# An attention stage in which weighing moves a step later, queries and keys are projected apart, and VectorE takes two copies from ScalarE

## The reference

```python
q = (inputs @ w_q.T).reshape(b, t, H, HD)      # b = 4, t = 256, H = 16 heads, HD = 16
k = (inputs @ w_k.T).reshape(b, t, H, HD)
v = (inputs @ w_v.T).reshape(b, t, H, HD)
scores = jnp.einsum('bqhd,bkhd->bhqk', q, k)
scores = jnp.where(causal, -jnp.inf, scores)
scale = jnp.float32(t) ** 0.5
attn = jax.nn.softmax(scores / scale, axis=-1)
ctx = jnp.einsum('bhqk,bkhd->bqhd', attn, v).reshape(b, t, D)
return ctx @ w_o.T + b_o
```

## Time and profile before

| what | value |
|---|---|
| median of three runs | 420.56 us |
| profiled execution | 420.87 us, span 419.1 us |
| PE busy | 380.4 us, 91% |
| DVE busy | 296.6 us, 71% |
| ACT busy | 256.6 us, 61% |
| POOL busy | 237.5 us, 57% |
| chain that ended last | PE 57%, DMA 16%, DVE 15%, ACT 3%, POOL 2% |

### The profile page before, as it was taken

The page is one execution under the profiler, slowest core; times in us unless marked ns, Lnnn a source line. Parts: engine busy times, 40 slices in busy tenths (PEclk is TensorE's granted clock), DMA queues, the critical chain, the costliest instruction groups (busy, mean ns, idle before and its releaser), DMA issues.

```text
span 419.1 us, 9185 instructions
## 1 busy us (share of the span) xinstructions
PE 380.4 (91%) x2732; PEld 309.0 (74%) x2733; DVE 296.6 (71%) x620; ACT 256.6 (61%) x640; POOL 237.5 (57%) x307
## 2 busy tenths in 40 slices
PE   7769999999999989788888988797899999999996
PEld 3548888888888867566666766473788888888885
DVE  6878999555666796887777757967466765566566
ACT  2837865656555546799888878621455556555552
POOL 5255445565567359567878668201555545745860
PEclk9999999999999999899999989999999999999999
DMA  7949921112111620466867587819721111112126
GB/s 253 399 125 391 379 97 54 52 38 75 50 50 38 238 77 0 76 114 116 151 117 129 103 108 145 139 20 305 238 96 55 53 62 52 50 50 57 43 96 231
DMA packets 70929, 51.57 MB, mean 123 GB/s; under 512 B 53104, under 2 KB 64624, under 8 KB 70640
## 3 DMA queue, kind: packets, MB, share of 16 engines
q1 hardware_dynamic: 66064, 36.99, 34.3%
q0 software_dynamic: 4544, 12.07, 9.3%
q10 hardware_dynamic: 288, 2.10, 1.3%
HBM read 29.37 MB, written 9.19 MB: 92 GB/s over the span
## 4 chain that ended last, share of the span: by engine, by line
PE 57%; DMA 16%; DVE 15%; issue 4%; ACT 3%; POOL 2%; SPq 1%; DVEq 0%; ACTq 0%; POOLq 0%
PE bank L1408 27%; PE bank L1430 13%; DMA pT<-parts 5%; DMA w_raw<-in_win_t 4%; PE bank L1418 4%; PE bank L1580 3%; DMA pT<-parts_late 3%; PE bank L1547 3%; PE bank L1384 2%; DMA w_out<-y_scratch 2%; DVE x L1097 2%; DMA y_scratch<-arena,scatter_row 2%; DVE neg_max L1200 1%; PE bank L1617 1%; DVE parts L1214 1%
## 5 line engine op out<-in xcount | busy, mean ns | idle before, releaser
L546 POOL DMA_INDIRECT arena<-xn_scratch,gather_row x46 | 49.6, 1078 | 68.1 <-PE bank L1384 46.7
L552 POOL DMA_INDIRECT y_scratch<-arena,scatter_row x42 | 62.5, 1488 | 37.1 <-ACT arena L715 35.3
L1408 PE MATMUL bank<-w_hi,xT_hi 128*128 x184 | 61.7, 416 | 0.4 <-ACT xT_hi L674 0.4
L1058 DVE TENSOR_TENSOR wo_lo<-w_out,wo_hi 128x1024 fp32r<-128x1024 f32 x46 | 56.3, 1224 | 3.8 <-PE bank L1430 2.2
L1063 DVE TENSOR_TENSOR gT_lo<-bank,gT_hi 128x512 fp32r<-128x512 f32 x46 | 31.7, 690 | 38.1 <-ACT gT_hi L689 38.1
L1408 PE MATMUL bank<-w_hi,xT_lo 128*128 x184 | 57.5, 393 | 0.0
L1408 PE MATMUL bank<-w_lo,xT_hi 128*128 x184 | 57.3, 392 | 0.0
L682 ACT ACTIVATE arena<-bank 128x512 f32<-128x512 f32 x46 | 27.6, 599 | 45.6 <-PE bank L1408 45.6
L627 POOL TENSOR_TENSOR k_head<-k_hi,head_mask 128x256 fp32r<-128x256 f32 x64 | 38.7, 626 | 24.3 <-PE bank L1581 24.3
L704 ACT ACTIVATE wo_hi<-w_out 128x1024 fp32r x46 | 48.8, 1061 | 5.1 <-issue 3.0
L1580 PE MATMUL bank<-k_head,xT_hi 128*128 128x256 f32 (+1 forms) x128 | 40.2, 395 | 7.7 <-DVE parts L1214 5.9
(11 more groups left out here) (196 smaller groups left out, 915.5 us busy)
## 6 DMA issues: line engine op xcount, KB each, us to landing
w_raw<-in_win_t SPq DMA_DIRECT2D x8, 1024.0 KB, 10.9
w_out<-in_wout_t SPq DMA_DIRECT2D x16, 512.0 KB, 7.6
w_out<-y_scratch SPq DMA_DIRECT2D x8, 512.0 KB, 5.3
xn_scratch<-arena ACTq DMA_DIRECT2D x2, 1024.0 KB, 6.2
x<-in_x SPq DMA_DIRECT2D x4, 256.0 KB, 3.4
out<-x SPq DMA_DIRECT2D x4, 256.0 KB, 2.2
arena<-xn_scratch,gather_row POOLq DMA_INDIRECT x46, 3.4
y_scratch<-arena,scatter_row POOLq DMA_INDIRECT x46, 3.0
```

The lines of the kernel that those rows point to most:

```text
L546: pool.indirect_dma_start(out=xb[j % 2][:, :], out_offset=None, in_=xn_dram, in_offset=bass.IndirectOffsetOnAxis(ap=gather_row[:, j:j + 1] ...
L552: pool.indirect_dma_start(out=y_dram, in_=y[j % 2][:, :], in_offset=None, out_offset=bass.IndirectOffsetOnAxis(ap=scatter_row[:, j:j + 1], ...
L1058: dve.tensor_tensor(wo_lo[:, :, :], w_out[:, bass.ds(e, 1), :, :].rearrange("p o c d -> p (o c) d"), wo_hi[u][:, :, :].bitcast(F32), ALU.s ...
L1408: last = pe.matmul(bank[2 * half + u][:, :], tok[u][:, k, :], wts[:, bass.ds(e, 1), k, half * H:(half + 1) * H], start=(part == 0 and k == ...
```

## The change

Weighing moves from the end of step s + 3 to step s + 4, ahead of the projections and the head scores; the last call of `step` gets a sixth inner step, and its matmuls on ones go from 6 to 5 a step. `chunk` is parted into `key_chunk` (steps 0 and 3, bank 7) and `query_chunk` (steps 1 and 4, bank 4). VectorE and no longer ScalarE makes `q_hi` and copies the turned context. The summing up of banks 5 and 6 is parted and lies in step 5 around the head maximum and head low part, with the reciprocal alone at the end of step 4. The turned context and the output projection use bank 4; the projection is parted around the tail scores of step 7. The values leave bank 4 and alternate between banks 5 and 6.

```diff
@@ -55,20 +55,20 @@
-VBANK = (3, 4, 5, 6, 5, 6, 5, 6)
+VBANK = (3, 5, 6, 5, 6, 5, 6, 5)
...
-CHUNK_STEP = (0, 3)
+KEY_STEP, QUERY_STEP = (0, 3), (1, 4)
...
-WARM_END = 6
+WARM_END = 5
@@ -378,7 +379,7 @@
-            return range(HPAIRS if new else SUM_STEP)
+            return range(HPAIRS if new else SLAG + 4)
@@ -791,13 +792,11 @@
-            def chunk(b, c):
...
-                act.wait_ge(qk_done, b * DK + (c + 1))
-                reach(act, head_scored, b * HPAIRS + (CPAIRS * (c + 1) - HPAIRS))
-                act.activation(k_hi[:, c, :], bank[7][:, SEQ:2 * SEQ], ACT.Copy).then_inc(k_hi_ready, 1)
-                act.activation(q_hi[c][:, :, :], bank[7][:, 0:SEQ].rearrange("p (q t) -> p q t", q=2), ACT.Copy,
-                               scale=1.0 / SEQ ** 0.5).then_inc(qk_hi_ready, 1)
+            def key_chunk(b, c):
...
+                act.wait_ge(k_done, b * DK + (c + 1))
+                reach(act, k_head_ready, b * HPAIRS + (CPAIRS * (c + 1) - HPAIRS))
+                act.activation(k_hi[:, c, :], bank[7][:, 0:SEQ], ACT.Copy).then_inc(k_hi_ready, 1)
@@ -839,18 +838,14 @@
                 for s in steps_of(new):
-                    if old and s == OUT_STEP:
-                        act.wait_ge(ctxT_done, b)
-                        act.activation(ctxT[:, :, :], bank[7][:, :].rearrange("p (k t) -> p k t", k=DK), ACT.Copy,
-                                       scale=1.0 / P_SCALE).then_inc(ctxT_ready, 1)
...
                         turn_out(1, (1,))
-                    if new and s in CHUNK_STEP:
-                        chunk(b, CHUNK_STEP.index(s))
+                    if new and s in KEY_STEP:
+                        key_chunk(b, KEY_STEP.index(s))
@@ -1181,14 +1176,21 @@
-            def chunk(b, c):
...
-                dve.wait_ge(qk_hi_ready, b * DK + (c + 1))
-                dve.tensor_tensor(k_lo[:, c, :], bank[7][:, SEQ:2 * SEQ], k_hi[:, c, :].bitcast(F32), ALU.subtract)\
+            def key_chunk(b, c):
...
+                dve.wait_ge(k_hi_ready, b * DK + (c + 1))
+                dve.tensor_tensor(k_lo[:, c, :], bank[7][:, 0:SEQ], k_hi[:, c, :].bitcast(F32), ALU.subtract)\
                     .then_inc(k_lo_ready, 1)
-                dve.scalar_tensor_tensor(q_lo[c][:, :, :], bank[7][:, 0:SEQ].rearrange("p (q t) -> p q t", q=2),
-                                         1.0 / SEQ ** 0.5, q_hi[c][:, :, :].bitcast(F32),
-                                         ALU.mult, ALU.subtract).then_inc(qk_ready, 1)
...
+            def query_chunk(b, c):
...
+                scaled = bank[4][:, 0:SEQ].rearrange("p (q t) -> p q t", q=2)
+                dve.wait_ge(q_done, b * DK + (c + 1))
+                reach(dve, head_scored, b * HPAIRS + (CPAIRS * (c + 1) - HPAIRS))
+                dve.tensor_scalar(q_hi[c][:, :, :], scaled, 1.0 / SEQ ** 0.5, None, ALU.mult).then_inc(q_hi_ready, 1)
+                dve.wait_ge(q_hi_ready, b * DK + (c + 1))
+                dve.scalar_tensor_tensor(q_lo[c][:, :, :], scaled, 1.0 / SEQ ** 0.5, q_hi[c][:, :, :].bitcast(F32),
+                                         ALU.mult, ALU.subtract).then_inc(q_ready, 1)
@@ -1214,19 +1216,23 @@
-            def add_up(b):
...
-                sums = row_sum[:, bass.ds(b - 1, 1), :, :].rearrange("p o q h -> p (o q) h")
+            def invert(b):
...
+                sums = row_sum[:, b - 1, :, :]
+                dve.wait_ge(high_ready, b * HEADS)
+                reach(dve, ctx_ready, b - 1)
+                dve.reciprocal(inv_sum[:, :, :], sums).then_inc(inv_ready, 1)
...
+            def add_up(b, qt):
...
                 dve.wait_ge(pv_done, b * HEADS)
-                for qt in range(2):
-                    dve.tensor_reduce(ctxv[:, qt, :, :], bank[5 + qt][:, :].rearrange("p (h w d) -> p h d w", w=2, d=HD),
-                                      AX_X, ALU.add).then_inc(ctx_summed, 1)
-                dve.reciprocal(inv_sum[:, :, :], sums).then_inc(inv_ready, 1)
+                dve.tensor_reduce(ctxv[:, qt, :, :], bank[5 + qt][:, :].rearrange("p (h w d) -> p h d w", w=2, d=HD),
+                                  AX_X, ALU.add).then_inc(ctx_summed, 1)
...
                 rows = x[:, bass.ds(b * 2 - 2, 2), :]
-                dve.tensor_tensor(rows, rows, bank[7][:, :].rearrange("p (q d) -> p q d", q=2), ALU.add)\
+                dve.tensor_tensor(rows, rows, bank[4][:, :].rearrange("p (q d) -> p q d", q=2), ALU.add)\
@@ -1247,18 +1253,28 @@
                 for s in steps_of(new):
-                    if old and s == SUM_STEP:
-                        add_up(b)
...
                         low(b, s, True)
+                    if old and new and s == SUM_STEP:
+                        add_up(b, 0)
...
                         maxima(b, s, False)
-                    if new and s in CHUNK_STEP:
-                        chunk(b, CHUNK_STEP.index(s))
+                    if new and s in KEY_STEP:
+                        key_chunk(b, KEY_STEP.index(s))
+                    if new and s in QUERY_STEP:
+                        query_chunk(b, QUERY_STEP.index(s))
...
                         low(b, s, False)
+                    if old and new and s == SUM_STEP - 1:
+                        invert(b)
+                    if old and new and s == SUM_STEP:
+                        add_up(b, 1)
+                    if old and new and s == OUT_STEP:
+                        dve.wait_ge(ctxT_done, b)
+                        dve.tensor_scalar(ctxT[:, :, :], bank[4][:, :].rearrange("p (k t) -> p k t", k=DK), 1.0 / P_SCALE, None,
+                                          ALU.mult).then_inc(ctxT_ready, 1)
@@ -1535,23 +1551,29 @@
-            def chunk(b, c):
...
-                if c:
-                    pe.wait_ge(qk_ready, b * DK + c)
-                else:
+            def key_chunk(b, c):
...
+                reach(pe, k_lo_ready, b * DK + c)
+                for k in range(DK):
+                    last = pe.matmul(bank[7][:, 0:SEQ], wk[:, k, c * P:(c + 1) * P], xnT[:, k, b * SEQ:(b + 1) * SEQ],
+                                     start=(k == 0), stop=(k == DK - 1))
+                last.then_inc(k_done, 1)
...
+            def query_chunk(b, c):
...
+                reach(pe, q_ready, b * DK + c)
+                if c == 0:
                     reach(pe, attn_added, b)
-                for w, to in ((wq, 0), (wk, SEQ)):
-                    for k in range(DK):
-                        last = pe.matmul(bank[7][:, to:to + SEQ], w[:, k, c * P:(c + 1) * P], xnT[:, k, bass.ds(b * SEQ, SEQ)],
-                                         start=(k == 0), stop=(k == DK - 1))
-                last.then_inc(qk_done, 1)
+                for k in range(DK):
+                    last = pe.matmul(bank[4][:, 0:SEQ], wq[:, k, c * P:(c + 1) * P], xnT[:, k, b * SEQ:(b + 1) * SEQ],
+                                     start=(k == 0), stop=(k == DK - 1))
+                last.then_inc(q_done, 1)
...
-                    reach(pe, v_rest_ready, t - 1 if t >= 4 else 0)
+                    reach(pe, v_rest_ready, t - 1 if t >= 3 else 0)
@@ -1566,7 +1588,7 @@
-                        pe.wait_ge(qk_ready, b * DK + (c + 1 - (DK if s < SLAG else 0)))
+                        pe.wait_ge(q_ready, b * DK + (c + 1 - (DK if s < SLAG else 0)))
@@ -1583,12 +1605,12 @@
-                g = b * HPAIRS + (s - SLAG - 3)
-                ago = s < SLAG + 3
-                turned = pT[(s - 1) % 2]
+                g = b * HPAIRS + (s - SLAG - 4)
+                ago = s < SLAG + 4
+                turned = pT[g % 2]
...
                 for hh in range(2):
-                    h = 2 * ((s - SLAG - 3) % HPAIRS) + hh
+                    h = 2 * ((s - SLAG - 4) % HPAIRS) + hh
@@ -1603,25 +1625,25 @@
-                    pe.wait_ge(qk_ready, b * DK + DK)
+                    pe.wait_ge(q_ready, b * DK + DK)
...
                         heads = ctxv[:, qt, c * HPC:(c + 1) * HPC, :].rearrange("p h d -> p (h d)")
-                        last = pe.transpose(bank[7][:, c * SEQ + qt * P:c * SEQ + (qt + 1) * P], heads, ident[:, :])
+                        last = pe.transpose(bank[4][:, c * SEQ + qt * P:c * SEQ + (qt + 1) * P], heads, ident[:, :])
...
-            def project_out(b):
+            def project_out(b, qt):
                 pe.wait_ge(ctxT_ready, b)
-                for qt in range(2):
-                    for c in range(DK):
-                        last = pe.matmul(bank[7][:, qt * D:(qt + 1) * D], ctxT[:, c, qt * P:(qt + 1) * P], wo[:, c, :],
-                                         start=(c == 0), stop=(c == DK - 1))
-                last.then_inc(o_done, 1)
+                for c in range(DK):
+                    last = pe.matmul(bank[4][:, qt * D:(qt + 1) * D], ctxT[:, c, qt * P:(qt + 1) * P], wo[:, c, :],
+                                     start=(c == 0), stop=(c == DK - 1))
+                if qt:
+                    last.then_inc(o_done, 1)
...
                 for s in steps_of(new):
-                    if old and s == OUT_STEP + 1:
```

(34 more changed lines are left out.)

## The result

| | before | after |
|---|---|---|
| median | 420.14 us (419.31 to 420.96, 4 runs) | 431.0 us (430.12 to 431.98, 4 runs) |
| profiled execution | 420.87, span 419.1 | 430.97, span 429.2 |
| batch 1, 2, 3, us from T0 to T0 | 25.02, 25.39, 27.28 | 30.26, 26.69, 27.03 |
| last call, T0 to the start of routing | 23.37 | 26.32 |

The routing starts with VectorE's first row that writes `chosen` (284.98 us before, 295.23 after). The changed kernel is slower: ratio 1.0259, interval [1.0227, 1.0291]. The forecast was 421.9 us, with a range of 416.8 to 425.8. The direction was the likeliest one, the size was far outside the range.

What follows compares the result with a forecast made beforehand. No engine is full; the order of hand-overs bounds the kernel. Terms -0.3+0.67+0.57+0+0.4 = +1.34 us on the profiled 420.87 give 422.2, and 421.9 as median, 0.31 lower; range 416.8 to 425.8 us.

Steps and rivals of the forecast that it cites:

- The walk of batch 2: Third attention batch, tail-score starts T0 to T7 added up from durations: next T0 at 25.95 us, before 25.39, +0.57.
- VectorE's copies: Query high parts, 0.41 us plus 0.03 wait each, and turned context, 0.60 us, moved from ScalarE, priced by two-input rows.
- Transposes "hidden": Later weighing hides the 3.9 us transposes: two steps must last 4.5 us, shortest two are 5.06; batch 2 loses 0.51.
- the forecast's own signs of being wrong: A batch under 25 us, the division less than 4 us after T5, or waits for pT in batches 1 to 3.
- Batch 3, "one fall kept": Fourth batch: walked 25.95 us plus one kept fall of TensorE's clock, 1.33, gives 27.28, as before: change 0.
- Last batch +0.4: Last call: VectorE starts 0.35 us later and the last transpose follows a weighing that itself waits for one: +0.4 us.
- my upper bound: Last batch's term: bounds 0 and +1.5 us, the upper one for a transpose of 5 us.
- First batch -0.3: First batch: step 3 sheds query work of two engines, -0.3 us, bounds -0.8 (no slow clock) and +0.5 (work in step 4).
- the forecast's 1.34: Summed change over the first batch, batches 1 to 3 and the last batch: +1.34 us.
- batch 1 (+0.67, measured +5.24): Second batch, starting without VectorE's late maximum: 25.69 us, before 25.02, so +0.67.
- transposes still late: Rival, all batches: with the longest landing, 5.4 us, two steps must last 6.0; +3.1 us, 423.7; chance 0.08.
- the clock falls in each batch: Rival, steps 5 and 6: TensorE's clock falls three times by 1.33 us, not once; +4.0, 424.6 us; chance 0.18.

Runs made afterwards that it cites:

- warmed_all: Changed kernel plus matmuls on ones before step 6's weighing and step 7's projection, in the first batch and in the last call: 428.7 us, 1.0189.
- scores_first: Changed kernel with GpSimd's step 7 masks ahead of the division and the output projection's first half behind step 7's tail scores: 426.5 us, 1.0124.
- first_fill: first_later plus six matmuls on ones behind the weighing in step 5 of the first batch: 418.35 us, 0.9943.
- first_later: Changed kernel; old weighing, sums, last call; first projection half behind step 7's tail scores; query parts before head maximum, except first batch's step 4: 418.63 us, 0.9942.

## Why the prediction was wrong

By its steps:

- **The walk of batch 2** (its masks end at 23.22, not 23.26, which changes nothing) gave T1 to T7 as 2.88, 6.92, 9.45, 12.06, 14.88, 17.98, 23.34 and the next T0 at 25.95. Measured: 2.98, 7.22, 9.78, 12.48, 15.38, 18.55, 23.94, 26.69. Each place where a wait was named held it: T2 ended by the query low part (T1 to T2 4.24, forecast 4.04), division 2.58 us idle, T5 to T7 8.56 (forecast 8 to 9). It is undersized by 0.74 us a batch, mostly in the four steps with half a projection: there VectorE gets the head scores 2.97 to 2.99 us after T, where I had 2.80. The weighing starts 0.89 to 0.91 after the tail scores, not 0.82, and the head scores reach VectorE 1.62 after the half projection's start, not 1.53; the weighing's 0.45 held.
- **VectorE's copies**, right: 0.41 for a query high part, and its low part starts 0.45 after it (forecast 0.41 and 0.03). The context took 0.69, as the 512-column rows do. By the Trainium skill ("VectorE: DVE Perf Modes", Why PSUM operands drop a tier) the one-input copy from PSUM gets no faster rate; the trace agrees, 0.41 us against 0.42 for the two-input one.
- **Transposes "hidden"**: wrong in part. In batch 1 T0 to T1 and T4 to T5 were 0.48 and 0.66 longer than in batch 2, each with TensorE waiting for pT (0.60 and 0.69); in batch 3 T1 to T2 0.37. I used the median landing of 3.9 us; the longest was 5.4 in both kernels. Waits for pT stood among the forecast's own signs of being wrong. And they were credited to the moved weighing, while the other edits remove them without it.
- **Batch 3, "one fall kept"**: there was none (27.03 against 25.95 walked); but batch 1, the first batch and the last call each had one. That batch 3 came out near its forecast (-0.25, forecast 0) is luck: the walk was 0.74 short and transposes added 0.34, and the 1.33 of the fall did not come.
- **Last batch +0.4**: +2.95. The last transpose was issued at T0 + 10.16 us, before at T0 + 8.64; that is 1.5, my upper bound. The rest, 1.43, I put down to the fall of the clock at 284 us, which I had not counted on; at full clock until 288 us warmed_all took only 0.8 less than the changed kernel, so the split is not settled. The order of the last call alone is not the loss: scores_first has it too, and took 23.75 us, +0.38 on before, with the last transpose at T0 + 9.09 and no fall. The forecast left out how the end of batch 3 sets when these transposes are issued.
- **First batch -0.3**: +1.0 with what lies ahead of it. Between T6 and T7 (3.10 us, with the clock low; first_fill 2.54 at full) about 0.6 is the clock.

Summed over the 8.8 us beyond the forecast's 1.34: undersized walk 2.5 (1.00, 0.73 and 0.74 in batches 1 to 3); transposes 2.6 (1.14, 0.34, and 1.52 less the 0.4 forecast); clock 2.9 (2.21, 0.56 and 1.43, less the 1.33 kept in batch 3); the rest, 0.8, is scattered. These are differences of single profiles; the split between transposes and clock is good to a microsecond or two.

The terms that failed are batch 1 (+0.67, measured +5.24) and the last batch (+0.4, measured +2.95), 7.1 of the 8.8 us. Both were added up with transposes at their median landing and with the clock of the kernel before. The step behind it is the one that treated late transposes and a lower clock as rivals with a price each, of which one would come true: the rivals "transposes still late" and "the clock falls in each batch" were both partly true at once, and the range, drawn about single cases, did not hold their sum.

What the experiments add: the moved weighing, with what moves with it, is the part that costs (3.1% without the rest; the rest without it 0.2%, an interval that holds no change). The walk had its place, steps 5 and 6. About 1.0 us a batch is left of it in the best orders tried; the remainder hangs on the orders about step 7, on the last call and on the clock.

## What to carry to other kernels

A loop over hand-written orders is worth checking edit by edit: here one moved step, with what followed it, cost all, and the others alone cost nothing that can be told. When a sum has several terms that can each go wrong the same way, longer gaps, later transfers and a lower clock, they can do so together, and the range must hold their sum. Work that a later order leaves to the end of a batch (sum, divide, turn, copy, project) goes behind the scores that keep the other engines fed, not ahead of them.

## What the hardware showed that I had not expected

TensorE's busy time just before does not tell a fall of its clock: after 2.79 us of work in 4 the grant went to 0.57 at 206 us, after 3.27 in 4 to 0.64 at 284, while after 2.71 in 4 it stayed at 1.00 in the kernel before. Two kernels that differ by six matmuls on ones in the first batch show it best, first_fill and then first_later, in batch 1:

```profile
200.00:204.00 4.00, 2.55 (x29) 1.67 (x27) 3.95 (x10) 2.84 (x12) 3.44 (x7) 1.00 0.70 133
```

```profile
200.00:204.00 4.00, 2.54 (x28) 1.61 (x26) 3.81 (x9) 2.98 (x13) 3.43 (x7) 1.00 0.53 102
204.00:208.00 4.00, 3.78 (x37) 2.97 (x37) 3.61 (x7) 3.92 (x15) 3.86 (x7) 1.00 0.64 125
```

After this first_fill was granted 0.57 in 204 to 208 us, first_later 1.00. And a fall that was filled away with matmuls on ones at 178 us was followed by one at 204 that the unfilled kernel did not have, and the time stayed.
